# A recurrence pipelined by one chunk, with the work beside it spread anew (linear attention with a gated FFN, eight cores)

## The reference

```python
xn = _layernorm(x, axis=-1)                      # x: 8 x 2048 x 2048
# recurrent attention, 16 heads of 128
q, k = rope(xn @ Wq), rope(xn @ Wk); v = xn @ Wv
beta = clip(sigmoid(xn @ Wg + bg), 0.8, 0.9995)  # one per token and head
pq, pk = elu(q) + 1.0, elu(k) + 1.0
def step(carry, inp):                            # over the 2048 tokens
    S = S * b_t + pk_t[:, None] * v_t[None, :]
    z = z * b_t + pk_t
    y_t = (pq_t @ S) / (sum(pq_t * z) + 1e-6)
s = y @ Wo + bo
# FFN on int32 weights: W = (wq - 128) * scale
g = silu(((silu(xn @ Wgate.T)) * (xn @ Wup.T)) @ Wdown.T)   # hidden 5632
out = x + s * g
```

## Time and profile before

| | us |
|---|---|
| median of the executions shown (two) | 5209.87 |
| lowest, highest | 5025.58, 5394.16 |
| profiled execution, its own time | 5028.59 |
| span of its slowest core (7) | 5027.0 |
| spans of the eight cores | 4952.4 to 5027.0 |
| granted PE clock, mean of a core | 0.856 to 0.862 of full speed |

### The profile page before, as it was taken

How to read it: one execution, slowest core, us unless ns; L and a number is a source line. 1 busy time by engine, 2 the same in 40 slices (tenths; PEclk the granted TensorE clock), 3 DMA queues, 4 the chain that set the end, 5 groups by cost and what they waited for, 6 DMA issues and landing times.

```text
span 5027.0 us, 43951 instructions; the slowest of 8 cores (4952.4 to 5027.0 us)
## 1 busy us (share of the span) xinstructions
PE 3232.3 (64%) x15056; PEld 1474.3 (29%) x15056; DVE 965.3 (19%) x1702; ACT 528.2 (11%) x1021; POOL 639.3 (13%) x721
## 2 busy tenths in 40 slices
PE   0004777868643668657776787758824888638888
PEld 0001333323221333323333343323411333213333
DVE  1233435353511111111111111111110000000000
ACT  0110122222210111101110111101100000000000
POOL 0101243333310000000000000000010000200000
PEclk9997898999876888888888888879957999869998
DMA  7662132323257443453435334363166444664443
GB/s 149 161 158 48 36 79 46 75 47 73 50 109 165 104 101 95 105 119 98 105 90 121 85 83 96 91 98 97 46 113 129 121 120 121 127 138 107 119 130 92
DMA packets 697787, 508.55 MB, mean 101 GB/s; under 512 B 426976, under 2 KB 629728, under 8 KB 691424
## 3 DMA queue, kind: packets, MB, share of 16 engines
q0 software_dynamic: 69360, 181.49, 16.9%
q1 hardware_dynamic: 458736, 162.73, 15.2%
q10 hardware_dynamic: 169472, 161.52, 12.2%
HBM read 337.83 MB, written 176.16 MB: 102 GB/s over the span
## 4 chain that ended last, share of the span: by engine, by line
PE 47%; DMA 18%; DVE 10%; SPq 8%; POOL 7%; issue 6%; ACT 3%; ACTq 1%; DVEq 0%; POOLq 0%
PE pb L712 13%; PE pb L720 10%; PE pb L1025 10%; SPq L971 5%; PE pb L950 5%; PE pb L570 4%; DMA raws<-wqg 4%; DMA raws<-wqu 4%; DMA raws<-wqd 3%; POOL swp L602 3%; DMA yTm<-yt_sp 3%; DMA xb<-x 2%; DVE tmp L608 2%; DVE tmp L616 2%; PE pb L841 2%
## 5 line engine op out<-in xcount | busy, mean ns | idle before, releaser
L712 PE MATMUL pb<-xnT,wgT 128*128 128x512 bf16 x2816 | 764.1, 433 | 31.5 <-DMA wgT<-wg_sp 31.5
L570 PE MATMUL pb<-ws,xnT 128*128 128x512 bf16 x2880 | 665.7, 392 | 118.5 <-DVE tmp L597 118.4
L720 PE MATMUL pb<-xnT,wuT 128*128 128x512 bf16 x2816 | 638.4, 380 | 17.9 <-DMA wuT<-wu_sp 17.9
L1025 PE MATMUL pb<-wdT,guTm 128*128 128x512 bf16 x2464 | 534.1, 379 | 0.0
L570 PEld LDWEIGHTS pb<-ws,xnT 128*128 128x128 bf16 x2880 | 284.4, 100 | 498.3 <-issue 193.7
L712 PEld LDWEIGHTS pb<-xnT,wgT 128*128 128x128 bf16 x2816 | 299.2, 109 | 418.5 <-issue 201.5
L950 PE MATMUL pb<-wos,yTm 128*128 128x512 bf16 x960 | 269.9, 451 | 186.9 <-DMA yTm<-yt_sp 186.9
L720 PEld LDWEIGHTS pb<-xnT,wuT 128*128 128x128 bf16 x2816 | 276.0, 98 | 351.7 <-issue 20.8
L1025 PEld LDWEIGHTS pb<-wdT,guTm 128*128 128x128 bf16 x2464 | 241.2, 98 | 290.6
L729 POOL TENSOR_TENSOR gub<-upsb,gsb 128x512 bf16<-128x512 bf16 x88 | 101.1, 1149 | 1466.3 <-ACT upsb L726 1466.3
L467 PE MATMUL pb<-xnT,wgb 128*16 128x512 bf16 x64 | 20.1, 484 | 410.0 <-DMA xnT<-xn_sp 396.0
(11 more groups left out here) (107 smaller groups left out, 2152.0 us busy)
## 6 DMA issues: line engine op xcount, KB each, us to landing
guTm<-gu_sp ACTq DMA_DIRECT2D x64, 704.0 KB, 9.1
raws<-wqg POOLq DMA_DIRECT2D x11, 2048.0 KB, 17.7
wg_sp<-raws POOLq DMA_DIRECT2D x11, 2048.0 KB, 8.6
raws<-wqu POOLq DMA_DIRECT2D x11, 2048.0 KB, 16.5
wu_sp<-raws POOLq DMA_DIRECT2D x11, 2048.0 KB, 8.9
gu_sp<-gub ACTq DMA_DIRECT2D x176, 128.0 KB, 2.1
raws<-wqd POOLq DMA_DIRECT2D x16, 1408.0 KB, 11.7
wd_sp<-raws POOLq DMA_DIRECT2D x16, 1408.0 KB, 5.7
```

The source lines that it names most:

```text
L570: P.mm_group([(lambda e, k=k, m=m, sl=sl, pbank=pbank: e.matmul(pb[pbank][:, 0:512], xnT[:, k * L + m * 128:k * L + (m + 1) * 128], wslot[ ...
L712: P.mm_group([(lambda e, k=k, t=t, tb=tb, sl=sl: e.matmul(pb[6][:, 0:512], wgT[sl][:, k * FS + t * 128:k * FS + (t + 1) * 128], xnT[:, k * ...
L720: P.mm_group([(lambda e, k=k, t=t, tb=tb, sl=sl: e.matmul(pb[7][:, 0:512], wuT[sl][:, k * FS + t * 128:k * FS + (t + 1) * 128], xnT[:, k * ...
L1025: e.matmul(pb[pbank][:, 0:DDS], guTm[msl][:, kh * 256 + mi * 128:kh * 256 + (mi + 1) * 128], wdT[j][:, kh * DDS:(kh + 1) * DDS], start=(kh ...
```

## The change

The body of a chunk is cut in two. phase_A(c) holds A and the mask; phase_rest(g, c) holds all that follows. In the loop over chunks, the loads and phase_A of chunk c are now followed by phase_rest of chunk c-1; the last chunk's phase_rest stands behind the loop. A of odd chunks goes to pb6 in place of pb0. The mask is emitted ahead of the job behind A, where it stood behind it. The jobs are placed anew: one behind A, one behind the numerator, one behind the store of ytb (ahead of L855), and one at the end of phase_rest unless c%4 is 3.

```diff
--- before.py
+++ after.py
@@ -772,34 +772,29 @@
                     if NS > 1:
                         emit_span_loads(1)
                     cur["span"] = min(1, NS - 1)
-                for c in range(NC):
-                    sl = c % 2
+                def phase_A(c):
                     cp = c % 2
-                    bkA = 0
-                    bkN = 1
-                    dco = 0 if cp == 0 else 8
-                    zco = 32 if cp == 0 else 40
-                    Am_, dsb_, rrow_, nsb_, ytb_ = Am[cp], dsb[cp], rrow[cp], nsb[cp], ytb[cp]
-                    if c % 2 == 0:
-                        emit_preps_until(cur["prep"] + 1)
-                    P.dma("se", lambda e, c=c, sl=sl, g=g: e.dma_start(
-                        vch[sl][:], v_sp[c * 128:(c + 1) * 128, g * HG * 128:(g + 1) * HG * 128]),
-                        reads=[v_spB[c][g]], writes=[vchB[sl]], sem=f"dvc{sl}")
-                    P.dma("se", lambda e, c=c, sl=sl, g=g: e.dma_start(
-                        hch[sl][:], kh_sp[c * 128:(c + 1) * 128, g * HG * 128:(g + 1) * HG * 128]),
-                        reads=[kh_spB[c][g]], writes=[hchB[sl]], sem=f"dhc{sl}")
+                    bkA = 0 if cp == 0 else 6
+                    Am_ = Am[cp]
                     P.mm_group([(lambda e, hl=hl, c=c, bkA=bkA: e.matmul(
                         pb[bkA][:, hl * 128:(hl + 1) * 128],
                         kTg[:, hl * L + c * 128:hl * L + (c + 1) * 128],
                         qTg[:, hl * L + c * 128:hl * L + (c + 1) * 128],
                         start=True, stop=True)) for hl in range(HG)],
                         reads=[qTgB, kTgB], writes=[pbB[bkA]])
-                    emit_ffn(1)
                     P.op("ve", lambda e, Am_=Am_, bkA=bkA: e.tensor_tensor(
                         Am_[:].rearrange("p (h j) -> p h j", h=HG),
                         pb[bkA][:, 0:HG * 128].rearrange("p (h j) -> p h j", h=HG),
                         maskf[:, None, :].broadcast_to([128, HG, 128]), ALU.mult),
                         reads=[pbB[bkA], maskB], writes=[AmB[cp]])
+
+                def phase_rest(g, c):
+                    sl = c % 2
+                    cp = c % 2
+                    bkN = 1
+                    dco = 0 if cp == 0 else 8
+                    zco = 32 if cp == 0 else 40
+                    Am_, dsb_, rrow_, nsb_, ytb_ = Am[cp], dsb[cp], rrow[cp], nsb[cp], ytb[cp]
                     numer_fns = []
                     for hl in range(HG):
                         h = g * HG + hl
@@ -852,6 +847,7 @@
                     P.dma("se", lambda e, c=c, g=g, ytb_=ytb_: e.dma_start(
                         yt_sp[c, :, g * HG * 128:(g + 1) * HG * 128], ytb_[:]),
                         reads=[ytbB[cp]], writes=[yt_spB[c][g]], sem=f"dyt{c % 2}")
+                    emit_ffn(1)
                     P.mm_group([(lambda e, hl=hl, sl=sl: e.matmul(
                         pb[5][:, hl * 128:(hl + 1) * 128], hch[sl][:, hl * 128:(hl + 1) * 128],
                         vch[sl][:, hl * 128:(hl + 1) * 128], start=True, stop=True))
@@ -884,6 +879,24 @@
                         st_b[:, g * HG * 129:(g + 1) * HG * 129],
                         st_f[:, g * HG * 129:(g + 1) * HG * 129], AF.Copy),
                         reads=[stfB], writes=[stbB])
+                    if c % 4 != 3:
+                        emit_ffn(1)
+
+                for c in range(NC):
+                    sl = c % 2
+                    if c % 2 == 0:
+                        emit_preps_until(cur["prep"] + 1)
+                    P.dma("se", lambda e, c=c, sl=sl, g=g: e.dma_start(
+                        vch[sl][:], v_sp[c * 128:(c + 1) * 128, g * HG * 128:(g + 1) * HG * 128]),
+                        reads=[v_spB[c][g]], writes=[vchB[sl]], sem=f"dvc{sl}")
+                    P.dma("se", lambda e, c=c, sl=sl, g=g: e.dma_start(
+                        hch[sl][:], kh_sp[c * 128:(c + 1) * 128, g * HG * 128:(g + 1) * HG * 128]),
+                        reads=[kh_spB[c][g]], writes=[hchB[sl]], sem=f"dhc{sl}")
+                    phase_A(c)
+                    emit_ffn(1)
+                    if c > 0:
+                        phase_rest(g, c - 1)
+                phase_rest(g, NC - 1)
             emit_ffn(len(ffn_jobs))
             emit_preps_until(len(prep_jobs))
         P.barrier()
```

## The result

The changed kernel is faster, by less than forecast. The ratio of its time to that of the kernel before is **0.9758, 95% interval 0.9706 to 0.9811**: 2.4% faster, where I had forecast 3.3%. That it is faster is clear of the interval; that it is faster by 2% is not, and the 0.967 of the forecast lies outside it. The medians over all executions are 5184.38 us of 11, beside 5110.26 of 10 for the kernel before; the executions that count took 4903 to 4943 us, inside the range of 4805 to 4975. Against the 5028.6 us on which the sum was built, 2.4% is 122 us, where the sum had 164.

What follows compares the result with a forecast made beforehand. PE was the engine to follow, its largest wait 325.0 us for DVE to write Am. Terms -203 -8 +37 -11 +14 +15 +7 -15 = -164 from 5028.6 gave 4865 us, -3.3%, range 4805 to 4975.

Steps and rivals of the forecast that it cites:

- term 1: PE's waits behind weight-block preps in the third stage: 316.6 us before, 114 after, -203; five 1.68 us waits go too, -8.
- term 2: A of odd chunks in pb6 makes the gate group wait for DVE's mask: +37 us over 24 chunks, bounds 25 and 108.
- term 4: SP's span load ahead of group 1's qTg, +15 us (0 to 18); last boundary's kTg wait less covered, +7 (0 to 9).
- terms 3 and 5: Chunks without jobs: -11 and +14 us; clock, fewer gate groups slowed after prep waits: -15 us (-24 to +20).
- the 7.4 for a chunk with jobs: Third stage: us per filled chunk without its jobs' time, from 435 us over 58.7 chunks; 11.3 chunks go to 8.65.
- some 14 fewer such waits at 1.1: Gate groups behind prep waits of 9 to 16 us: fewer slowed by a lower clock, -15 us.
- The 1.7 that I called the most: Most us a gate group loses to the lower clock after a prep wait: 5.30 in place of 3.62.
- Rival 1: Wait behind blocks only moves: every prep is of the late-issue kind, load no earlier; 4984 us, chance 0.15.
- rival 3: All waits behind preps vanish as POOL's loads run ahead and blocks land sooner: another 96 us off, 4769 us, chance 0.08.
- case A: Chunk's first job odd, gub on DVE; load issued as before, wait 3.9 us less: 12.2 (gate/up blocks) or 5.8 (down).
- case B: Chunk's first job even; load issued 7.5 us earlier, PE meets DVE at dsb: down blocks nothing left, gate/up 3 us each.
- Rival 2: Bank 6 takes the gain back at the 24 odd A's, 9.7 us each, 233 instead of 37: 5061 us, chance 0.07.

Runs made afterwards that it cites:

- without job d: The changed kernel without the job at the end of a chunk, so three jobs a chunk; ratio to the kernel before 1.0036.
- flipped parity: The changed kernel with gub of odd jobs formed by POOL and of even jobs by DVE; 12 gub waits, 106.9 us in the mean, no ratio given.
- the run with bank 0: The changed kernel with A of every chunk in pb0, nothing else different; ratio to the kernel before 0.9658.
- the engine bound to the place: The changed kernel with gub on POOL for a chunk's first and third job, on DVE for second and fourth; ratio to the kernel before 0.9568.
- the version put together: The changed kernel with weight-block load and finish separated, every A in pb0, jobs spread 48, 48, 40, 40 over the groups; ratio 0.9299, median 4680.25 us.
- the version with the mask first: The kernel before with weight-block load and finish separated, vch and hch loaded a chunk ahead, mask ahead of the job behind A; 4763.99 and 4709.24 us.

## Why the prediction was right and wrong

**The waits behind blocks (term 1): right.** 118 us are left where 114 were forecast, 76 in nine waits for gub and the rest at dsb and the start. The single values hold as well: on core 2 gub with gate/up blocks 10.60 to 13.41 (12.2 forecast), with down blocks 5.01 to 6.37 (5.8). Of the 9 us by which the term is short, 5 come from core 7's 325, on which the sum was made, where the mean of the cores is 320. The runs without job d and with flipped parity test the counting itself, at 199 for 203 and at 107 for 105.

**Bank 6 (term 2): right, 6 us small.** 43 of waits in place of 37, and few slow groups behind them: of the 178 gate groups in this place whose records are whole, over the cores, 14 took over 4 us (up to 6.55) and the others about 3.6. What the bank costs beyond its waits is open, as the run with bank 0 shows.

**Boundaries (term 4): 10 us small.** The first is 17 longer (15 forecast, bounds 0 and 18), the last 9 (7 forecast), and the second, which I had set at 0, is 5.5 longer. That one is a single core: core 5 waits 61.7 us there, the other seven 24.3 to 31.2, where all eight waited 19.3 to 39.4 before. (The 25.25 us that the sum has for wgT is of all 16 transposes; the line of the earlier trace rows holds 13 of them.)

**Bare chunks and clock (terms 3 and 5): wrong, and the largest miss.** A bare chunk is as forecast, 8.77 us for 8.65, and 16 of them. But the 7.4 for a chunk with jobs is a remainder that holds its slow gate groups too, so terms 3 and 5 share the clock, and only their sum of +3 - 15 = -12 can be held against the trace. The account of the stage closes without a remainder (means over the cores, first A to last numerator): -202 + 43 + 32 are the terms above; besides, the wait for rrow is 12 less (the prediction had it unchanged), that for vch or st_b 23 more, those for the weights and smaller ones 2 more, the gate groups' time 35 less, **the up groups' time 23 more**, that of all other matmuls 13 more, as eleven more chunks are bare and run at half the clock. That is +14 where I had -12, and -113 in all. Of the 51 us between 164 and 113, 9, 6 and 10 are in terms 1, 2 and 4, and 26 here.

Without the up groups it would be -9 for -12. So the step that failed is "some 14 fewer such waits at 1.1": it took a block's wait to slow the gate group behind it, as before, and had no price for the up groups on which the waits now fall. The rows show it, first before, then after:

```profile
2476.50 5.42 PE L712 MATMUL pb<-xnT,wgT 128*128 128x512 bf16 x16
2481.76 3.62 PE L720 MATMUL pb<-xnT,wuT 128*128 128x512 bf16 x16
```

```profile
2454.27 5.81 PE L720 MATMUL pb<-xnT,wuT 128*128 128x512 bf16 x16 [13.41 <-DVE gub L733]
...
2534.97 6.42 PE L720 MATMUL pb<-xnT,wuT 128*128 128x512 bf16 x16 [6.07 <-DVE gub L733]
```

Before, all 25 gate groups behind a numerator that had waited for a block were slow, 5.42 us in the mean of the six cores with whole records, and of the up groups only the one behind the first wait for wuT. Now all nine up groups behind a gub wait are slow, 5.83 in the mean over the cores where 3.62 is usual: 9 x 2.2 = 20 us that no row of waits holds. With the engine bound to the place there is no gub wait, and these slow groups are gone with it. The 1.7 that I called the most was too little for both kinds. All matmuls together took 1551 us of the stage before and 1553 after: what the clock gave back on the gates went to the up groups and to the bare chunks, and the whole gain is idle time (622 to 507 us).

**The rivals.** Rival 1 (4984) and rival 3 (4769) failed for the change itself, because 9 blocks are case A and 12 case B; each has since been seen in a run of its own kind, in the one without job d (all case A) and, nearly, in the one with the engine bound to the place (all case B, but 48 us left, which rival 3 had at nothing). Rival 2 fell by the change's own rows, 1.9 us per odd chunk. None of my rivals named what was found by cutting the block, that the removed wait covered vch.

**Where the large gain lay.** The change took 2.4% of the 7.0% that this stage had to give by the means tried here. It moved the consumer away from the stalled queue; cutting the load from its use takes the stall out of the queue, and with the waits that it uncovers treated as well it needs no running ahead.

Open: 7 us at the first boundary, the 14 us lost outside the stage (33 in the version put together), the bank's price beyond its waits, and the time of the version with the mask first, for which two executions are too few.

## What to carry to other kernels

When an engine that takes its work in order shows an operation idle "behind a DMA", look at what stands behind it in the queue: that is who pays, and putting the operation one period after its load is worth more than moving the payer. Before you remove a wait, ask which other transfer or engine it covers, and read that one's time to landing, not its wait: 111 us came out from under 320. Where work alternates between engines by a counter, count the parity at each place before changing how many jobs a period has: here it decides between no gain (1.0036) and 2.4%. And price a stall by its wait and by the slow group behind it.

## What the runs showed of the hardware

Small loads landed late beside large ones: the 128 KB of vch in 10.6 us in the median when issued within 3 us behind a block's load of 1.4 to 2 MB, in 2.4 otherwise (the kernel before; 9.1 and 2.5 with the block cut). And large ones landed later once PE no longer stood still for them. DMA issues from 1600 to 2440 us with the block cut, in the kernel before, core 4 (KB each, us to landing):

```profile
raws<-wqu POOLq DMA_DIRECT2D x6, 2048.0 KB, 25.2
...
vch<-v_sp ACTq DMA_DIRECT2D x27, 128.0 KB, 3.1
```

The blocks land in 25.2 us where they took 16.5: I take it, without a run that shows it, that more transfers run beside it now that PE doesn't stand still for it. PE did not wait for those 9 us, since the finish comes two chunks later.

SP can be held by a single transpose: the four of qTg hold it for 35.20 us in the rows above where the four of kTg take 14.13, though the tiles are of one size. The third of the four takes 25.08 of it, the others 1.94 to 4.04. SP wasn't waiting for qTg to come free, since the first two had gone out by then; what held the third is not shown.
